# Two lanes of a decoder planned anew: other TensorE prices in the planner of the engines' queues

## The reference

```python
x = x + L0_attn(norm(x))          # sparse attention, 16 heads
x = x + L0_xattn(norm(x), ctx)    # cross attention
x = x + L0_ffn(norm(x))           # two layers: local attention with 8 heads, then a gated MLP
x = x + L1_attn(norm(x))          # causal attention, 16 heads of 8
x = x + L1_xattn(ctx, norm(x))
x = x + L1_ffn(norm(x))           # 8 experts, the best 2 of each row
x = x + L2_attn(norm(x))          # window, compressed and selected keys
x = x + L2_xattn(norm(x), ctx)
x = x + L2_ffn(norm(x))           # 8 small experts
x = x + L3_attn(norm(x))          # selective scan over 512 steps, 16 states
x = x + L3_xattn(norm(x), ctx)    # difference of two attentions
x = x + L3_ffn(norm(x))           # gated MLP with quantised operands
```

## Time and profile before

| | us |
|---|---|
| median of 3 runs | 2509.95 |
| lowest, highest of them | 2505.46, 2511.8 |
| profiled execution, device time | 2501.56 |
| its span, first to last instruction | 2499.8 |
| mean granted TensorE clock | 0.825 of 2.4 GHz |

### The profile page before, as it was taken

One profiled execution on the slowest core, in us unless ns is written; L12 is line 12 of the kernel. 1 busy time (PEld: TensorE's weight loads), 2 busy tenths in 40 slices (PEclk: granted clock), 3 DMA queues, 4 the chain that ended last, 5 costly groups with the idle time before them and its releaser, 6 DMA issues. The chain is left out here.

```text
span 2499.8 us, 31121 instructions
## 1 busy us (share of the span) xinstructions
PE 1946.5 (78%) x11378; PEld 1099.6 (44%) x11378; DVE 1644.7 (66%) x3698; ACT 1030.2 (41%) x1610; POOL 584.6 (23%) x520
## 2 busy tenths in 40 slices
PE   4787887878787877799899767778876766689973
PEld 2453634445363232367676545555532222233321
DVE  6666657575666454453536797895469998985566
ACT  1236464564644343343333223233245345334561
POOL 0003323241321010010001353531025534631000
PEclk8888999999898677899999778866567776798975
DMA  4002122130302000000000000000000000000000
GB/s 158 1 1 64 35 52 47 26 72 18 81 1 88 1 1 1 1 22 1 1 1 1 1 1 1 1 1 1 0 0 1 0 0 0 0 1 1 1 5 13
DMA packets 19223, 43.77 MB, mean 18 GB/s; under 512 B 5323, under 2 KB 7935, under 8 KB 18175
## 3 DMA queue, kind: packets, MB, share of 16 engines
q1 hardware_dynamic: 19071, 41.78, 5.9%
HBM read 16.59 MB, written 1.05 MB: 7 GB/s over the span
## 5 line engine op out<-in xcount | busy, mean ns | idle before, releaser
L2185 PE MATMUL lane_banks<-l_attn_lane_hc,base 128*128 128x512 f32 x256 | 176.8, 809 | 98.4 <-DVE l_attn_lane_hc L2336 98.4
L2261 POOL TENSOR_TENSOR l_attn_lane_u<-l_attn_lane_xp,l_attn_lane_bn 128x512 f32<-128x512 f32 x128 | 177.1, 1409 | 207.7 <-ACT l_attn_lane_bn L2237 203.5
L2327 DVE TENSOR_TENSOR_SCAN l_attn_lane_h<-l_attn_lane_da,l_attn_lane_u 128x512 f32<-128x512 f32 x128 | 187.4, 1493 | 7.7 <-POOL l_attn_lane_u L2261 3.9
L1577 ACT ACTIVATE l_ffn_lane_hT<-lane_banks,weights 128x512 f32<-128x512 f32 x128 | 88.0, 687 | 153.3 <-PE lane_banks L1533 153.0
L543 POOL TENSOR_SCALAR lane_next_rstd<-lane_next_mv 128x4 f32<-128x4 f32 x48 | 12.1, 253 | 587.3 <-DVE lane_next_mv L529 587.2
L1385 ACT ACTIVATE l_attn_lane_ex<-lane_banks 128x1024 f32<-128x1024 f32 (+3 forms) x128 | 87.2, 702 | 139.9 <-PE lane_banks L1343 139.6
L2185 PEld LDWEIGHTS lane_banks<-l_attn_lane_hc,base 128*128 128x128 f32 x256 | 57.6, 246 | 178.9 <-DVE l_attn_lane_hc L2336 139.6
L1555 PEld LDWEIGHTS lane_banks<-weights,l_ffn_lane_hT 128*128 128x128 f32 x1024 | 121.4, 193 | 24.3 <-issue 21.1
L1623 DVE SCALAR_TENSOR_TENSOR l_ffn_lane_eo<-lane_banks,l_ffn_lane_sel,l_ffn_lane_eo 128x128 f32<-128x128 f32 x224 | 63.0, 344 | 103.9 <-PE lane_banks L1555 103.5
L1555 PE MATMUL lane_banks<-weights,l_ffn_lane_hT 128*128 128x128 f32 x1024 | 124.2, 278 | 5.6 <-DVE l_ffn_lane_eo L1623 4.4
L2237 ACT ACTIVATE l_attn_lane_bn<-lane_banks 128x512 f32<-128x512 f32 x64 | 38.0, 595 | 203.5 <-PE lane_banks L2179 200.8
(11 more groups left out here) (528 smaller groups left out, 4699.4 us busy)
## 6 DMA issues: line engine op xcount, KB each, us to landing
f_attn_lane_work<-f_attn_lane_work SPq DMA_DIRECT2D x256, 64.0 KB, 2.0
weights<-packed SPq DMA_DIRECT2D x1, 4564.5 KB, 19.5
f_attn_lane_vb<-f_attn_lane_va SPq DMA_DIRECT2D x8, 512.0 KB, 4.5
f_attn_lane_vb<-f_attn_lane_va SPq DMA_DIRECT2D x8, 384.0 KB, 5.9
weights<-packed SPq DMA_DIRECT2D x1, 2320.0 KB, 8.5
weights<-packed SPq DMA_DIRECT2D x1, 2091.0 KB, 12.9
out<-x SPq DMA_DIRECT2D x4, 256.0 KB, 2.2
weights<-packed SPq DMA_DIRECT2D x1, 897.0 KB, 9.1
```

Source lines behind the costliest of these rows:

```text
L1577: act.activation(hT[:, n % 2, c, :], ps(c), ACT.Relu, bias=w("m1_b1", b, b + 1)).then_inc(*s.up("hidden_ready"))
L2185: pe.matmul(ps(2 + c), w("ident"), hc[:, c, :], start=(n == 1), stop=(n == NS)).then_inc(*s.up("state_added"))
L2261: g.tensor_tensor(u[:, i % 3, :], dtx[:, c, :], bn[:, n % 2, :], ALU.mult).then_inc(*s.up("u_ready"))
L2327: v.tensor_tensor_scan(h[:, c, :], da[:, i % 3, :], u[:, i % 3, :], 0.0, ALU.mult, ALU.add).then_inc(*s.up("scanned"))
```

## The change

`Meter.matmul` and `Meter.transpose` get other formulas. No unit, no instruction, no buffer and no wait of the device program is edited; the prices of the other engines stay. Whatever differs on the chip comes from another `order`.

```diff
     def matmul(self, out, lhsT, rhs, start, stop):
-        rows = lhsT.shape[0]
-        share = 0.3 if rows <= 32 else 0.6 if rows <= 64 else 1.0
-        return self.work(0.05 + share * width(out) * (0.0006 if rhs.dtype == BF16 else 0.0018))
+
+        share = 0.25 if out.shape[0] <= 32 else 0.5 if lhsT.shape[0] <= 32 else 1.0
+        return self.work(share * (0.17 + width(out) * (0.0006 if rhs.dtype == BF16 else 0.00095)))

     def transpose(self, out, in_, identity):
-        return self.work(0.06 + 0.0009 * width(out))
+        return self.work(0.3)
```

## The result

The changed kernel takes 2550.06 us (median of 4 runs, 2549.76 to 2551.39), the kernel before beside it 2507.7 us (4 runs, 2503.78 to 2511.8). The ratio is 1.0172, interval [1.0155, 1.0188]: 42 us slower. Forecast were +15 us; the sign is right, the size is not.

A forecast was written before the change was run, and what follows sets the result against it. No single engine was taken to bound the kernel: PE, DVE or queue order and chains, by stage. Terms 5 + 8 + 2 = +15 us gave 2516.6 for the profiled execution, median 2525; 8-in-10 range 2465 to 2570.

The forecast's parts named there:

- The planner's picture is somewhat worse than before: Planner's prices: one error mended (32-output-row products), others made; PE about as large in sum but in the wrong places.
- f0, forecast +5 (-10 to +10): Local attention: dearer PE and more uneven pieces in turn push block pairs towards the slow rhythm, +5 us.
- 32 pairs, about half at each: Local attention's block pairs, half at 5.15 and half at 5.8 us; all good -10 us, all bad +10.
- l1_attn, forecast +8 (-24 to +24): l1_attn's eight set pairs of 31 to 37 us: a third of the way to the bad end, +8 us.
- The experts and the difference attention, forecast +2 (-5 to +10): Both PE's own; keyed pieces of the difference attention stay too cheap and its apply becomes so, +2 us.
- l2_attn and l3_attn, forecast 0 (-15 to +15): DVE's stages, in the plan too, with its prices held right: 0 us, bounds a third of DVE's idle time.
- The tail, 0 (-15 to +15): Last 98 us, DVE at 64%: 0 us, bounds if the lanes end closer together or further apart.
- Table loads: Rival: 16 more ACT table loads from mixing lanes' Ln and Exp, +20 us; 2564 with bad ends; over 2550, 0.07.
- No difference: Rival: lanes still alternate on PE and single stages cancel, or the order hardly changes; 2510, within 7.5 us; chance 0.20.
- The faster rival: Mended price lets one lane's row maxima run beside the other's keyed phase in l1_attn, -24 us; 2479 or 2495; chance 0.36.
- the likeliest case: Whole kernel slower by a few tenths to 1.5%, own range 2518 to 2550 us; chance 0.37.
- the case of all bad ends: Local attention and l1_attn at their bad ends plus table loads, 2564 us; it or table loads, over 2550: 0.07.

The follow-up runs named there:

- f0_m: Kernel before, with the new prices for products only, in the local-attention block (f0) alone; median 2535.62 us, ratio 1.0143.
- after_swap: Changed kernel, with the other lane's maximum put between a block's subtract and its sum in DVE's finished order where allowed; 2534.1 us, ratio 1.0127.
- after_actdma: Changed kernel, with the two copies that shift the values by half a block issued by ACT instead of SP; 2530.35 us, ratio 1.0087.
- after_fix: Changed kernel with two repairs: maxima moved between subtract and sum on DVE, value copies issued by ACT instead of SP; 2509.03 us, ratio 1.0017.
- outs32: Kernel before, with only products of at most 32 output rows priced at a quarter of the old formula; 2497.75 us, ratio 0.9969.
- f0_t: Kernel before, with the new price for transposes only, in the local-attention block (f0) alone; 2498.89 us, ratio 0.9977.
- f0_old: Changed kernel, with the old prices in the local-attention block (f0) alone; 2502.23 us, ratio 0.9986.

## Why the prediction was right and wrong

**The direction, and why.** "The planner's picture is somewhat worse than before" held where it counted, in f0, and through the products' price: f0_m shows it without the transposes (+27.7 in f0). That it is the dear small products, as the text named them, is likely but not shown apart. The reason was only argued then; now it can be followed to the queue. With a block at 5.9 us of PE in the plan instead of 3.9, the other lane's scores are late in the plan, so no maximum is ready when a subtract ends, and the sum is put next. This link is worked out from the planner's rule; the two repairs show what the order costs, not how the plan came to it. (The products of L967 are of 64 rows by 128 columns for all blocks but the first of a unit, not by 64; the prices of 0.19 and 0.29 are those of 128.)

**f0, forecast +5 (-10 to +10), measured +41.3.** This is the step that failed. I made the sum from the two rhythms of a pair of blocks, 5.15 and 5.8 us, "32 pairs, about half at each". The mechanism was there: two of a lane's four units were at the slow rhythm before, and all are now but for the first blocks of each. It cost +13.0, where +5 was taken and +10 was the bound. The windows answer to the earlier trace rows (eight blocks, 5.8 us a pair):

```profile
425.70:448.90 23.20, 18.73 (x296) 14.76 (x294) 17.06 (x32) 10.87 (x20) 8.33 (x9) 1.00 0.01 1
```

But the block phases were only 145 of 549 us, and the step left the rest without a term. "SP's issues are the same too" is true of their number; their order cost +19.2 us in the gap. The two lanes in near lockstep cost +15.7 in the feed-forward part and +5.2 at the attention's end, and gave back 8.2 in the chunks: 13.0 + 19.2 + 15.7 + 5.2 - 8.2 = 44.9. What these parts leave out, the stretches ahead of the first L1096 of a unit, went from 23.8 to 20.2, which makes the 41.3. (Of the chunks' 8.2 the order may be behind little: they differ by 6.5 with one order.) By cause, as the runs with one thing repaired have it: the reductions' order in the blocks 16 us (after_swap), SP's order in the gap 20 to 21 (after_actdma), both together all 41 (after_fix). The text named what it didn't price, "if the distance between the lanes grows"; it fell instead, and the bound of f0 should have had it in.

**l1_attn, forecast +8 (-24 to +24), measured -10.3.** Wrong in sign. I judged that the keyed pieces, now too dear, would outweigh the mended price; outs32 shows that the mended price alone gives nearly all of it (-9.2). L1444 in two windows, against 37 and 31 us in the earlier trace rows:

```profile
815.40:847.30 31.90, 11.35 (x8) 0.68 0.00 1
1000.10:1032.00 31.90, 11.36 (x8) 0.73 0.01 1
```

The rhythm is the good end that I had seen, in every set pair looked at. The rival's mechanism, lanes 10 us or more of a set apart, isn't it: they end the stage 1.5 us apart, and in the window of one set pair PE is busy 25.13 and DVE 14.93 of 32 us, not both over 75% (why the rhythm is better at 1.5 us wasn't followed to a queue):

```profile
848.00:880.00 32.00, 25.13 (x213) 9.65 (x212) 14.93 (x25) 11.75 (x18) 0.00 (x0) 0.73 0.00 1
```

**The experts and the difference attention, forecast +2 (-5 to +10), measured +6.1 and +7.5.** Together 13.6, over the bound. In the experts PE is busy for 95% of the stage, as before (96%), at a granted clock of 0.97 for 0.99; whether the order is behind that no run shows. The difference attention can't be read so closely from one execution, as the windows of that stage in f0_t show, a kernel whose order is that of before in this stage (184 us in the earlier trace rows):

```profile
2222.00:2396.00 174.00, 162.26 (x957) 62.30 (x955) 113.30 (x264) 100.43 (x125) 24.09 (x32) 0.96 0.00 1
```

The granted clock is 0.96 there and 0.90 in before, and PE's time is 10.6 us apart for the same work. So how much of the +7.5 is the order stays open.

**l2_attn and l3_attn, forecast 0 (-15 to +15), measured -0.3 and +8.4.** Within the bound; "its prices are right" was not: 1493 ns was a mean over mostly two lengths, 1.2 and 2.0 us, and agreed with the price of 1.48 by chance. Which scans are long is again a matter of order.

**The tail, 0 (-15 to +15), measured -10.2.** Counted from the mean of the lanes' ends it is half of their distance and 13.7 us more, in both kernels; the distance at the end is 10.1 us now and was 30.5. That much of the gain is a matter of where the stage before is said to end: by the windows it is 98 and 90.5 us. **Table loads:** this rival fell. The line of the logarithm has one fewer than in the earlier trace rows, all lines together 63 for 75:

```profile
L1021 ACT ACT_TABLE_LOAD x16 | 20.5, 1283 | 0.3
```

**The rivals and the range.** No difference fell by 42 us. The faster rival had half of l1_attn's price right (-10 for -24 to -12) and would need f0 untouched: f0_old, the change without f0, is at 0.9986. The measured time is inside the range for 8 in 10 and just over the likeliest case's own 2518 to 2550. What made the range wide enough was the case of all bad ends, though not by its reasons, and that is luck. The sign is luck in part too: of the three terms of the sum the largest, l1_attn's +8, was wrong in sign, and f0 outweighed it mostly by parts that had no term.

## What to carry to other kernels

When only an order changes, list every in-order queue and ask of each which waiting piece could now stand ahead of a ready one of the other lane, DMA issues first: in this kernel that was 19 of 41 us, on a queue that only issues DMAs. A rhythm seen in one phase bounds that phase, not its stage; cost the other phases too, and the distance between the lanes, which prices at the far end of the plan can change. Here it paid to repair the two bad places themselves, one in the finished order and one in who issues the copies (0.9937 with the one mended price); none of the other prices tried gave as much. And before a stage's difference is put down to an order, look at how far the same order varies there.

## What the runs showed of the hardware

The scan of 128x512 in float32 on DVE takes 1.2 us alone and 2.0 us beside a product of POOL on 128x512 (means of 69 and 39 scans of before), and the mean of POOL's product grew from 1409 to 1548 ns with more overlap. The Trainium skill (SBUF — State Buffer, section "SBUF: two separate sides") says that DVE, in an operation with two operands in SBUF, and GpSimd take a shared pair of ports in turn, one blocking the other. The trace agrees as to direction; the full length of POOL's product (median 1094 ns in before) on top of the scan would be 2.3 us, and the mean of the overlapped scans is 1.97, so not every such scan was held up for all of it.

Two kernels with one order in a stage can differ there by 10 us with nothing but the granted clock seen to differ: the difference attention (184 and 174 us at 0.90 and 0.96), and f0 (554, 549 and 541 us at 0.91, 0.92 and 0.96).

A table load on ACT takes 1283 ns. The changed kernel has 16 at the logarithm's line (L1021), one for each of its 16 stretches of Ln, and 16 at the Exp behind them (L1027).
